# Building the quadratic feature map behind the window attention instead of ahead of it, in a fused attention and mixture-of-experts layer

## Chip, cores and metric

The kernel runs on the 8 cores of one Trainium2 chip. Each core takes one of the 8 sequences (4096 tokens of width 1024) and all weights; the cores exchange nothing. The metric is the device time in microseconds (us) of the slowest core. Times in the profile are of that core, one execution.

## What is computed

One layer: an attention block, a layer norm, an expert block, a layer norm. The attention block has two kinds of heads side by side on the same q, k and v: a causal linear attention on a feature map phi, and a softmax attention over a window of 65 tokens.

```python
def taylor_feature_map(x):            # x: [..., 16]  ->  [..., 153]
    iu, ju = jnp.triu_indices(d)
    scale = jnp.where(iu == ju, 0.5, 1.0 / math.sqrt(2.0))
    quad = x[..., iu] * x[..., ju] * scale
    return jnp.concatenate([ones, x, quad], axis=-1)
h = rmsnorm(x, norm_w)
q, k, v = h @ Wq, h @ Wk, h @ Wv                    # 16 heads of 64
q_phi, k_phi = taylor_feature_map(q @ Wqf), taylor_feature_map(k @ Wkf)
lin = linear_attention_causal(q_phi, k_phi, v)      # chunks of 128, carried state kv
win = sliding_window_attention(q, k, v)             # keys t-64 to t
x = layernorm(x + x + concatenate([lin, win]) @ Wout)
# then, with E=8 experts and TOP_K=2 of them per token:
# h0 = x w0, h1 = x w1, out = sum over chosen e of g_e * (h0 * silu(h1)) w2
x = layernorm(x + moe(x))
```

## The kernel before

A core works in four quarters of 1024 tokens. A quarter has two superchunks of 512 tokens (`superchunk`, line 364) and then the expert part (`phase_B`, line 854) over its 1024 tokens. A superchunk normalises four chunks of 128 tokens, transposes them, makes q, k and v of all four (192 matmuls of 128x512), and calls `chunk_attn` (line 469) for each of its four chunks. So there are 32 calls.

`Plan.op` (line 49) appends one instruction to the queue of its engine. An engine runs its queue strictly in the order in which the program emitted it. DVE, ACT and POOL instructions also wait for the one before on their own engine, and `after=[...]` names what else an instruction waits for, by counting semaphores. So the order in the source is the order on every engine. All rows of the profile have line 90, that of the helper; they are told apart by tile and shape. Most tiles of the attention part are carved out of one buffer and so are all named `arena`.

A call of `chunk_attn` emits, in this order:

- POOL copies q of this chunk into `q_pad` (lines 485 to 489); it waits for the last scores of the window attention of the chunk before (`prev_qpad_read`).
- PE projects q and k of the chunk on the 16 features (lines 491 to 504), DVE copies them out as `qf_tm` and `kf_tm`.
- `emit_tail` (line 769) for the chunk before: DVE copies the state to bf16, PE transposes the concatenated heads, ACT evacuates them, PE runs the output projection into `pbA` (32 matmuls 128x512), DVE adds it to the residual `t1`, and the layer norm follows in four passes of 1024 columns on ACT with small steps of DVE between the first ones. The first chunk of a quarter has no tail ahead of it.
- The phi build (lines 511 to 557): DVE scales `qf_tm` and `kf_tm` by 1/sqrt(2) into `qf_h` and `kf_h`, sets the ones, copies the linear terms, and multiplies the 15 groups of mixed terms, for q and k at once. POOL makes the 32 groups of squares (the diagonal terms, each 128x16), which wait for the second scaling `t_sc`; an `engine_nop` closes them and gives the token `t_phig`.
- The window attention (lines 561 to 625), in four groups of four heads: scores of the chunk's own keys into `pb3` and of the keys before into `pb6` (PE), two exponentials (ACT), two masks (POOL, `maskC` and `maskP`), the products with v into `pbB` (PE), a reciprocal and a multiplication (DVE). The exponentials of a group wait for the products of the group before (`prev_yw`), since `eC` and `eP` exist once.
- The linear attention (lines 630 to 724), again in four groups: PE transposes phi of q and of k into `pT`, which waits for `t_phi` and `t_phig`, ACT evacuates it, PE makes the scores, DVE masks them, PE makes the output and the state update, DVE normalises and adds.

The lines that set the hand-overs named above:

```python
t_sc = tsc("vector", self.kf_h[:, :], self.kf_tm[:, :], INV_SQRT2, None, ALU.mult, inc="v")
OP("gpsimd", "tensor_tensor", k3d[:, :, off:off + 1], khh3[:, :, i:i + 1],
   khh3[:, :, i:i + 1], ALU.mult, after=[t_sc, self.prev_kd])
teCm = OP("gpsimd", "tensor_tensor", ..., ALU.mult, after=[teC])
ttr = OP("tensor", "transpose", ..., after=[t_phi, t_phig, self.lr["pT"], self.prev_yl])
```

Of the kernel before, what the change touches and what calls it, by code (L numbers as in the profile page):

```python
# [14 lines left out]
NH = 16  # L15
FEAT = 16
# [7 lines left out]
INV_SQRT2 = float(1.0 / np.sqrt(2.0))  # L24
# [102 lines left out]
class Builder:  # L127
# [341 lines left out]
    def chunk_attn(self, S, c, C, tk_q, tk_k, tk_v):  # L469
        OP, tsc = self.OP, self.tsc  # L470
# [5 lines left out]
        def kslice(h_or_sl, width=128, prev=False, whole_slice=True, off=0):  # L476
# [10 lines left out]
           after=[tk_q[0], tk_q[1], self.prev_qpad_read])  # L487
# [3 lines left out]
        for sl in range(8):  # L491
# [6 lines left out]
                    after=[tk1], inc="v")  # L498
# [9 lines left out]
        self.emit_tail()  # L508
        if self.castage < 1:
            return  # L510
        tsc("vector", self.qf_h[:, :], self.qf_tm[:, :], INV_SQRT2, None, ALU.mult,
            after=[self.prev_phig])
        t_sc = tsc("vector", self.kf_h[:, :], self.kf_tm[:, :], INV_SQRT2, None,
                   ALU.mult, inc="v")

        k3d = self.kphi.rearrange("p (h w) -> p h w", h=NH)
        q3d = self.qphi.rearrange("p (h w) -> p h w", h=NH)
        ktm3 = self.kf_tm.rearrange("p (h w) -> p h w", h=NH)
        qtm3 = self.qf_tm.rearrange("p (h w) -> p h w", h=NH)
        khh3 = self.kf_h.rearrange("p (h w) -> p h w", h=NH)  # L520
        qhh3 = self.qf_h.rearrange("p (h w) -> p h w", h=NH)
        OP("vector", "memset", k3d[:, :, 0:1], 1.0, after=[self.prev_kd])
        OP("vector", "memset", q3d[:, :, 0:1], 1.0)
        OP("vector", "tensor_copy", k3d[:, :, 1:17], ktm3[:, :, :])
        OP("vector", "tensor_copy", q3d[:, :, 1:17], qtm3[:, :, :])
        import dataclasses as _dc
        def _two_sided(ap_k, ap_q):
            d = ap_q.offset - ap_k.offset
            return bass.AP(tensor=ap_k.tensor, offset=ap_k.offset,
                           ap=[list(p) for p in ap_k.ap[:1]] +  # L530
                              [[d, 2]] + [list(p) for p in ap_k.ap[1:]])
        off = 17
        t_phiv = None
        for i in range(FEAT):
            n = FEAT - i
            if n > 1:
                outv = _two_sided(k3d[:, :, off + 1:off + n],
                                  q3d[:, :, off + 1:off + n])
                in0v = _two_sided(
                    khh3[:, :, i:i + 1].broadcast_to([128, NH, n - 1]),  # L540
                    qhh3[:, :, i:i + 1].broadcast_to([128, NH, n - 1]))
                in1v = _two_sided(ktm3[:, :, i + 1:FEAT], qtm3[:, :, i + 1:FEAT])
                t_phiv = OP("vector", "tensor_tensor", outv, in0v, in1v, ALU.mult,
                            inc=("v" if i == FEAT - 2 else None))
            off += n
        off = 17
        for i in range(FEAT):
            n = FEAT - i
            OP("gpsimd", "tensor_tensor", k3d[:, :, off:off + 1],
               khh3[:, :, i:i + 1], khh3[:, :, i:i + 1], ALU.mult,  # L550
               after=[t_sc, self.prev_kd])
            OP("gpsimd", "tensor_tensor", q3d[:, :, off:off + 1],
               qhh3[:, :, i:i + 1], qhh3[:, :, i:i + 1], ALU.mult)
            off += n
        t_phig = OP("gpsimd", "engine_nop")
        self.prev_phig = t_phig
        t_phi = t_phiv

        if self.castage < 2:
            return  # L560
        win_toks = []
        for hg in range(4):
            hs4 = [4 * hg + j for j in range(4)]
            tsC = None
            for j, h in enumerate(hs4):
                tsC = OP("tensor", "matmul", self.pb3[:, 128 * j:128 * (j + 1)],
                         kslice(h // 2), self.q_pad[:, 128 * h:128 * (h + 1)],
                         start=True, stop=True,
                         after=[tqp, tk_k[0], tk_k[1], self.lr["pb3"]],
                         inc=("t" if j == 3 else None))  # L570
            teC = OP("scalar", "activation", self.eC[:, :], self.pb3[:, :],
                     AF.Exp, scale=WIN_SCALE, after=[tsC, self.prev_yw], inc="s")
            teCm = OP("gpsimd", "tensor_tensor",
                      self.eC.rearrange("p (j w) -> p j w", j=4),
                      self.eC.rearrange("p (j w) -> p j w", j=4),
                      self.maskC[:, :].unsqueeze(1).broadcast_to([128, 4, 128]),
                      ALU.mult, after=[teC])
            self.lr["pb3"] = teCm
            tePm = None
            if C > 0:  # L580
                tsP = None
                for j, h in enumerate(hs4):
                    tsP = OP("tensor", "matmul",
                             self.pb6[:, 128 * j:128 * (j + 1)],
                             kslice(h // 2, prev=True),
                             self.q_pad[:, 128 * h:128 * (h + 1)],
                             start=True, stop=True,
                             after=[self.lr["pb6"],
                                    self.ktail_tok if first_c else None],
                             inc=("t" if j == 3 else None))  # L590
                teP = OP("scalar", "activation", self.eP[:, :], self.pb6[:, :],
                         AF.Exp, scale=WIN_SCALE, after=[tsP, self.prev_yw], inc="s")
                tePm = OP("gpsimd", "tensor_tensor",
                          self.eP.rearrange("p (j w) -> p j w", j=4),
                          self.eP.rearrange("p (j w) -> p j w", j=4),
                          self.maskP[:, :].unsqueeze(1).broadcast_to([128, 4, 128]),
                          ALU.mult, after=[teP])
                self.lr["pb6"] = tePm
            self.prev_qpad_read = tsP if C > 0 else tsC
            tyw = None  # L600
            for j, h in enumerate(hs4):
                tk = OP("tensor", "matmul", self.pbB[:, 512 + 65 * j:512 + 65 * (j + 1)],
                        self.eC[:, 128 * j:128 * (j + 1)], vr[:, 65 * h:65 * (h + 1)],
                        start=True, stop=(C == 0),
                        after=[teCm, tk_v[0], tk_v[1], self.lr["pbB"]],
                        inc=("t" if (C == 0 and j == 3) else None))
                if C > 0:
                    tk = OP("tensor", "matmul", self.pbB[:, 512 + 65 * j:512 + 65 * (j + 1)],
                            self.eP[:, 128 * j:128 * (j + 1)],
                            vprev[:, 65 * h:65 * (h + 1)],  # L610
                            start=False, stop=True,
                            after=[tePm, self.vtail_tok if first_c else None],
                            inc=("t" if j == 3 else None))
                tyw = tk
            self.prev_yw = tyw
            zwin = self.pbB[:, 512:772].rearrange("p (j w) -> p j w", w=65)[:, :, 64:65]
            rcw = OP("vector", "reciprocal", self.smal[:, 16:20], zwin.squeeze(2),
                     after=[tyw], inc="v")
            c3 = self.concat.rearrange("p (half h w) -> p half h w", half=2, w=64)
            tnw = OP("vector", "tensor_tensor", c3[:, 1, 4 * hg:4 * hg + 4, :],  # L620
                     self.pbB[:, 512:772].rearrange("p (j w) -> p j w", w=65)[:, :, 0:64],
                     self.smal[:, 16:20].unsqueeze(2).broadcast_to([128, 4, 64]),
                     ALU.mult, after=[rcw, self.prev_ct], inc="v")
            self.lr["pbB"] = tnw
            win_toks.append(tnw)
        if self.castage < 5:
            return
        concat_last = None
# [101 lines left out]
    def OP(self, *a, **k):  # L730
        return self.pl.op(*a, **k)

    def tsc(self, eng, out, in0, s1, s2, op0, op1=None, after=(), inc=None, accum=None):
        if accum is not None:
            return self.OP(eng, "tensor_scalar", out, in0, s1, None, op0, op1,
                           accum_out=accum, after=after, inc=inc)
        if op1 is None:
            return self.OP(eng, "tensor_scalar", out, in0, s1, None, op0,
                           after=after, inc=inc)
        return self.OP(eng, "tensor_scalar", out, in0, s1, s2, op0, op1,  # L740
                       after=after, inc=inc)
# [444 lines left out]
```

How the kernel before makes its waits and increments, by code:

```python
        def f(e, waits=waits, meth=meth, args=args, kw=kw, incname=incname, incn=incn):  # L87
            for s, v in waits:
                e.wait_ge(sems[s], v)
            r = getattr(e, meth)(*args, **kw)
            if incname is not None:
                r.then_inc(sems[incname], incn)
# [16 lines left out]
        def f(e, waits=waits, fn=fn):  # L109
            for s, v in waits:
                e.wait_ge(sems[s], v)
            fn(e)
```

## Time and profile before

| what | us |
|---|---|
| median of 4 runs | 9538.18 |
| lowest and highest of them | 9407.78, 9975.75 |
| the profiled execution | 9407.96 |
| its span, slowest core (the others 9390.2 to 9403.5) | 9406.4 |
| PE busy in the span | 7036.7 (75%) |
| ACT, DVE, POOL busy | 2686.1, 1830.2, 871.6 |

Busy time of PE is an upper bound of its work, as matmuls are pipelined. The shares are means over two very different parts, attention and experts, so that a stage has to be read by itself. In the rows below, a row of the timeline has the start in us from the span's start, the length in us, the engine, line and operation, output and inputs with shapes, the number of merged instructions, and in brackets how long the engine had been idle before and what released it.

### The profile page before, as it was taken

How to read it: one execution, taken by the hardware profiler on the slowest of the kernel's cores; microseconds unless marked ns; L12 is line 12 of the kernel's file. 1: busy time of each engine (PE TensorE's matmuls, PEld its weight loads, DVE VectorE, ACT ScalarE, POOL GpSimd, SP SyncE). 2: the span in 40 equal slices, each digit the busy share in tenths (PEclk: the TensorE clock that was granted, in tenths of full speed). 3: DMA queues.
4: the chain of work that ended last, by engine and by line, in shares of the span. 5: the costliest groups of instructions: out<-in, count | busy, mean ns of one | idle time of the engine just before them, and what ended most of it. 6: DMA issues, size and time to landing. Idle time of an engine off the chain costs nothing.

```text
span 9406.4 us, 104878 instructions; the slowest of 8 cores (9390.2 to 9406.4 us)
## 1 busy us (share of the span) xinstructions
PE 7036.7 (75%) x37091; PEld 3423.8 (36%) x37091; DVE 1830.2 (19%) x4145; ACT 2686.1 (29%) x3885; POOL 871.6 (9%) x1533
## 2 busy tenths in 40 slices
PE   3344799999434479999944448999993444999998
PEld 1222344444222234444422223444442222444443
DVE  2222211111222221111122222111112222111111
ACT  1222233334222223333422222333342222233334
POOL 1212000000121100000012110000001111000000
PEclk8565899999656589999965659999996565999999
DMA  3000554643300054463420006355342001535442
GB/s 59 1 10 1 86 80 61 96 64 64 63 1 10 1 92 74 71 95 55 72 56 1 10 5 99 62 81 85 57 83 43 4 2 17 94 55 91 74 69 60
DMA packets 244417, 493.81 MB, mean 52 GB/s; under 512 B 14528, under 2 KB 14528, under 8 KB 243904
## 3 DMA queue, kind: packets, MB, share of 16 engines
q0 software_dynamic: 225472, 453.02, 31.0%
q1 hardware_dynamic: 18432, 34.09, 1.2%
q8 instruction: 305, 5.00, 0.2%
q14 instruction: 208, 1.70, 0.1%
HBM read 923.32 MB, written 16.78 MB: 100 GB/s over the span
## 4 chain that ended last, share of the span: by engine, by line
PE 71%; ACT 9%; POOL 7%; issue 5%; DVE 5%; DMA 2%; DVEq 0%; ACTq 0%; POOLq 0%; SPq 0%
PE pb L90 40%; PE pbA L90 16%; PE pbB L90 11%; ACT arena L90 8%; POOL arena L90 7%; PE pT L90 4%; DVE arena L90 3%; DMA arena<-x 1%; DVE t L90 1%; ACT t L90 1%; DVE smal L90 1%; DMA arena<-gb 1%; ACT smal L90 0%; DVEq L89 0%; ACTq L89 0%
## 5 line engine op out<-in xcount | busy, mean ns | idle before, releaser
L90 PE MATMUL pb<-arena 128*128 128x512 bf16 (+2 forms) x19328 | 3896.7, 364 | 305.2 <-ACT arena L90 257.7
L90 PEld LDWEIGHTS pb<-arena 128*128 128x128 bf16 (+1 forms) x19328 | 1850.5, 103 | 2323.4 <-issue 393.5
L90 ACT ACTIVATE arena<-pb,arena 128x512 bf16<-128x512 f32 x2048 | 1407.3, 687 | 2147.9 <-PE pb L90 2050.4
L90 PE MATMUL pbB<-arena 128*128 128x512 bf16 (+1 forms) x5504 | 1088.7, 342 | 1104.3 <-POOL arena L90 973.5
L90 PE MATMUL pbA<-arena 128*128 128x512 bf16 x6656 | 1554.7, 395 | 50.3 <-ACT arena L90 42.2
L90 DVE TENSOR_TENSOR arena<-arena 128x512 bf16<-128x512 bf16 (+13 forms) x1536 | 654.0, 426 | 3150.7 <-ACT arena L90 2951.7
L90 PEld LDWEIGHTS pbB<-arena 128*128 128x128 bf16 x5504 | 527.6, 104 | 1655.8 <-issue 1172.5
L90 PEld LDWEIGHTS pbA<-arena 128*128 128x128 bf16 x6656 | 670.9, 101 | 903.8 <-issue 180.1
L90 PE MATMUL pT<-idbf,arena 128*128 128x128 bf16 (+1 forms) x3072 | 415.7, 303 | 649.4 <-DVE arena L90 404.8
L90 ACT ACTIVATE arena<-pT 128x512 bf16<-128x512 bf16 (+1 forms) x576 | 368.7, 640 | 1269.6 <-PE pT L90 1245.8
L90 DVE TENSOR_TENSOR t<-t,arena 128x1024 f32<-128x1024 f32 x256 | 313.6, 1225 | 1553.7 <-ACT arena L90 1553.7
L90 PEld LDWEIGHTS pT<-idbf,arena 128*128 128x128 bf16 (+1 forms) x3072 | 272.2, 130 | 764.0 <-issue 754.8
L90 POOL TENSOR_TENSOR arena<-arena 128x16 bf16<-128x16 f32 x1024 | 340.1, 332 | 1815.2 <-DVE arena L90 1670.7
L90 POOL DMA_DIRECT2D arena<-w0t x64 | 57.1, 893 | 4199.4 <-PE pb L90 3957.2
L90 ACT ACTIVATE arena<-pb 128x512 bf16<-128x512 f32 x252 | 150.5, 597 | 926.9 <-PE pb L90 912.6
L90 ACT ACTIVATE arena<-pbA,arena 128x1024 f32<-128x1024 f32 x128 | 142.6, 1114 | 720.1 <-PE pbA L90 719.4
L90 ACT ACTIVATE arena<-pbB,arena 128x1024 f32<-128x1024 f32 x128 | 142.6, 1114 | 701.9 <-PE pbB L90 700.4
L90 DVE TENSOR_TENSOR arena<-pb,maskL 128x512 bf16<-128x512 f32 x128 | 88.5, 691 | 702.1 <-PE pb L90 702.1
L90 ACT ACTIVATE arena<-t 128x1024 bf16<-128x1024 f32 x64 | 67.6, 1056 | 392.6 <-DVE t L90 392.6
L90 DVE CAST arena<-pbA 128x512 bf16<-128x512 f32 x192 | 132.9, 692 | 226.0 <-PE pbA L90 226.0
L90 POOL TENSOR_TENSOR arena<-arena,maskC 128x512 bf16<-128x512 bf16 x128 | 147.2, 1150 | 207.9 <-ACT arena L90 198.5
L90 ACT ACTIVATE arena<-t,smal 128x1024 bf16<-128x1024 f32 (+1 forms) x128 | 146.9, 1148 | 36.8 <-DVE smal L90 30.8
(84 smaller groups left out, 1755.7 us busy)
## 6 DMA issues: line engine op xcount, KB each, us to landing
arena<-w2t POOLq DMA_DIRECT2D x32, 4352.0 KB, 31.6
arena<-w0t POOLq DMA_DIRECT2D x64, 2048.0 KB, 18.2
arena<-w1t POOLq DMA_DIRECT2D x64, 2048.0 KB, 28.3
arena<-x SPq DMA_DIRECT2D x32, 512.0 KB, 3.7
out<-t SPq DMA_DIRECT2D x32, 512.0 KB, 2.7
arena<-wout POOLq DMA_DIRECT2D x6, 2048.0 KB, 55.9
arena<-wq POOLq DMA_DIRECT2D x4, 2048.0 KB, 17.8
arena<-wk POOLq DMA_DIRECT2D x4, 2048.0 KB, 33.3
```

The source lines that it names most:

```text
L90: r = getattr(e, meth)(*args, **kw)
```

## The change

The phi build moves from ahead of the window attention to behind it, as one block. No instruction, token or buffer is changed. The tail of the chunk before stays where it was, ahead of both.

```diff
@@ -508,54 +508,6 @@
         self.emit_tail()
         if self.castage < 1:
             return
-        tsc("vector", self.qf_h[:, :], self.qf_tm[:, :], INV_SQRT2, None, ALU.mult,
-            after=[self.prev_phig])
-        t_sc = tsc("vector", self.kf_h[:, :], self.kf_tm[:, :], INV_SQRT2, None,
-                   ALU.mult, inc="v")
...
-        t_phig = OP("gpsimd", "engine_nop")
-        self.prev_phig = t_phig
-        t_phi = t_phiv
-
         if self.castage < 2:
             return
         win_toks = []
@@ -623,6 +575,53 @@
                      ALU.mult, after=[rcw, self.prev_ct], inc="v")
             self.lr["pbB"] = tnw
             win_toks.append(tnw)
+        tsc("vector", self.qf_h[:, :], self.qf_tm[:, :], INV_SQRT2, None, ALU.mult,
+            after=[self.prev_phig])
+        t_sc = tsc("vector", self.kf_h[:, :], self.kf_tm[:, :], INV_SQRT2, None,
+                   ALU.mult, inc="v")
...
+        t_phig = OP("gpsimd", "engine_nop")
+        self.prev_phig = t_phig
+        t_phi = t_phiv
         if self.castage < 5:
             return
```

POOL's queue in the second chunk of the kernel, before. The two copies are `q_pad`, the 32 instructions of 128x16 the squares, `ISA` the nop behind them, and maskC and maskP the masks of the four groups; the last copies are those of the chunk after:

```order
L90 COPY arena<-arena 64x8x128 x2
L90 TENSOR_TENSOR arena<-arena 128x16 x32
L90 ISA
L90 TENSOR_TENSOR arena<-arena,maskC 128x512
L90 TENSOR_TENSOR arena<-arena,maskP 128x512
L90 TENSOR_TENSOR arena<-arena,maskC 128x512
L90 TENSOR_TENSOR arena<-arena,maskP 128x512
L90 TENSOR_TENSOR arena<-arena,maskC 128x512
L90 TENSOR_TENSOR arena<-arena,maskP 128x512
L90 TENSOR_TENSOR arena<-arena,maskC 128x512
L90 TENSOR_TENSOR arena<-arena,maskP 128x512
L90 COPY arena<-arena 64x8x128 x2
```

And the same stretch of POOL's queue now:

```order
L90 COPY arena<-arena 64x8x128 x2
L90 TENSOR_TENSOR arena<-arena,maskC 128x512
L90 TENSOR_TENSOR arena<-arena,maskP 128x512
L90 TENSOR_TENSOR arena<-arena,maskC 128x512
L90 TENSOR_TENSOR arena<-arena,maskP 128x512
L90 TENSOR_TENSOR arena<-arena,maskC 128x512
L90 TENSOR_TENSOR arena<-arena,maskP 128x512
L90 TENSOR_TENSOR arena<-arena,maskC 128x512
L90 TENSOR_TENSOR arena<-arena,maskP 128x512
L90 TENSOR_TENSOR arena<-arena 128x16 x32
L90 ISA
L90 COPY arena<-arena 64x8x128 x2
```

The squares and their nop moved from ahead of the first mask to behind the last one, and stand now between the masks and the next chunk's copies.

DVE's queue in the same chunk, now. The 128x1024 addition is the residual of the tail, the pairs on `pbB` are the four normalisations of the window, the rows from the scaling (TENSOR_SCALAR 128x256) on are the phi build:

```order
L90 TENSOR_TENSOR t<-t,pbA 128x1024
L90 TENSOR_SCALAR smal<-smal 128x1 x2
L90 RECIPROCAL smal<-pbB 128x4
L90 TENSOR_TENSOR arena<-pbB,smal 128x256
...
L90 RECIPROCAL smal<-pbB 128x4
L90 TENSOR_TENSOR arena<-pbB,smal 128x256
L90 TENSOR_SCALAR arena<-arena 128x256 x2
L90 MEMSET arena 128x16 x2
L90 CAST arena<-arena 128x16x16 x2
L90 TENSOR_TENSOR arena<-arena 128x2x16x15
```

Before, the rows from the scaling on stood directly behind the two small TENSOR_SCALAR of the layer norm, and the four pairs on `pbB` behind the last product. PE's and ACT's queues are the same before and now.

## Rows read from the trace of the kernel before

**Rows 1.** The page, granted TensorE clock in 40 slices of the span, in tenths

```profile
PEclk8565899999656589999965659999996565999999
```

**Rows 2.** Busy time by stage: PE, PEld, DVE, ACT, POOL, then PEclk, DMA share, GB/s

```profile
0.00:964.00 964.00, 391.38 (x2859) 232.41 (x2859) 253.85 (x583) 200.06 (x317) 181.97 (x353) 0.64 0.10 17
964.00:2352.00 1388.00, 1337.26 (x6248) 608.43 (x6249) 209.60 (x456) 442.89 (x613) 35.98 (x38) 0.98 0.49 76
```

**Rows 3.** Who waited for whom, whole span: us in total, times, longest us

```profile
PE pbB L90 <- POOL arena L90: 1001.4, 252, 22.4
```

**Rows 4.** Timeline, 413 to 432, a chunk with a tail ahead

```profile
413.23 10.00 PE L90 MATMUL pbA<-arena 128*128 128x512 bf16 x32 [1.32 <-ACT arena L90]
...
423.06 0.61 PE L90 MATMUL pb<-arena 128*128 128x128 bf16 x8
...
428.07 0.69 DVE L90 TENSOR_SCALAR arena<-arena 128x256 f32<-128x256 f32 x2
...
429.03 15.10 POOL L90 TENSOR_TENSOR arena<-arena 128x16 bf16<-128x16 f32 x32 [57.62 <-DVE arena L90]
...
430.19 8.13 DVE L90 TENSOR_TENSOR arena<-arena 128x480 bf16<-128x480 f32 x15
431.18 1.29 ACT L90 ACTIVATE arena<-pb 128x512 bf16<-128x512 f32 x2
```

**Rows 5.** Timeline, 444 to 462, the window attention of the same chunk

```profile
444.43 1.15 POOL L90 TENSOR_TENSOR arena<-arena,maskC 128x512 bf16<-128x512 bf16 x1 [0.29 <-POOLq L90]
...
445.72 0.21 PE L90 MATMUL pbB<-arena 128*128 128x65 bf16 x1 [22.05 <-POOL arena L90]
...
447.37 1.04 PE L90 MATMUL pb<-arena 128*128 128x128 bf16 x8
...
448.13 1.29 ACT L90 ACTIVATE arena<-pb 128x512 bf16<-128x512 f32 x2 [15.67 <-PE pb L90]
448.93 1.15 POOL L90 TENSOR_TENSOR arena<-arena,maskC 128x512 bf16<-128x512 bf16 x1 [2.07 <-ACT arena L90]
...
460.89 1.15 PE L90 MATMUL pT<-idbf,arena 128*128 128x128 bf16 x8
461.26 0.18 DVE L90 RECIPROCAL smal<-pbB 128x4 f32<-128x4 f32 x1 [3.80 <-PE pbB L90]
...
461.55 0.42 DVE L90 TENSOR_TENSOR arena<-pbB,smal 128x256 bf16<-128x256 f32 x1
```

**Rows 6.** Timeline, 7879 to 7893, the same place in the last such chunk

```profile
7879.06 1.29 ACT L90 ACTIVATE arena<-pb 128x512 bf16<-128x512 f32 x2
7892.31 1.15 POOL L90 TENSOR_TENSOR arena<-arena,maskC 128x512 bf16<-128x512 bf16 x1 [0.29 <-POOLq L90]
```

**Rows 7.** Timeline, 159 to 189, the first chunk, without a tail ahead

```profile
159.94 0.60 ACT L90 ACTIVATE arena<-pb 128x512 bf16<-128x512 f32 x1 [48.55 <-PE pb L90]
...
176.34 1.15 POOL L90 TENSOR_TENSOR arena<-arena,maskC 128x512 bf16<-128x512 bf16 x1 [0.30 <-POOLq L90]
...
186.99 2.20 POOL L90 COPY arena<-arena 64x1024 bf16<-64x1024 bf16 x2
...
187.29 1.15 PE L90 MATMUL pT<-idbf,arena 128*128 128x128 bf16 x8
...
187.95 0.42 DVE L90 TENSOR_TENSOR arena<-pbB,smal 128x256 bf16<-128x256 f32 x1
```

**Rows 8.** Busy time in stretches of 2 us, columns as in rows 2

```profile
424.00:426.00 2.00, 0.00 (x0) 0.00 (x0) 0.62 (x1) 1.15 (x2) 0.00 (x0) 1.00 0.00 0
426.00:428.00 2.00, 0.00 (x0) 0.00 (x0) 0.31 (x2) 1.24 (x2) 0.00 (x0) 0.50 0.00 0
...
430.00:432.00 2.00, 0.00 (x0) 0.00 (x0) 1.69 (x4) 1.82 (x3) 1.57 (x4) 0.50 0.00 0
...
440.00:442.00 2.00, 0.00 (x0) 0.00 (x0) 0.00 (x0) 0.00 (x0) 1.28 (x6) 0.50 0.00 0
```

**Rows 9.** Timeline of PE, 5437, the shortest output projection

```profile
5437.48 8.39 PE L90 MATMUL pbA<-arena 128*128 128x512 bf16 x32 [1.32 <-ACT arena L90]
```

More of the change, by code:

```diff
@@ L510, in chunk_attn @@
             return
-        tsc("vector", self.qf_h[:, :], self.qf_tm[:, :], INV_SQRT2, None, ALU.mult,
-            after=[self.prev_phig])
-        t_sc = tsc("vector", self.kf_h[:, :], self.kf_tm[:, :], INV_SQRT2, None,
-                   ALU.mult, inc="v")
[L516 to L554, printed above, removed]
-        t_phig = OP("gpsimd", "engine_nop")
-        self.prev_phig = t_phig
-        t_phi = t_phiv
@@ L625, in chunk_attn @@
             win_toks.append(tnw)
+        tsc("vector", self.qf_h[:, :], self.qf_tm[:, :], INV_SQRT2, None, ALU.mult,
+            after=[self.prev_phig])
+        t_sc = tsc("vector", self.kf_h[:, :], self.kf_tm[:, :], INV_SQRT2, None,
+                   ALU.mult, inc="v")
+        k3d = self.kphi.rearrange("p (h w) -> p h w", h=NH)
+        q3d = self.qphi.rearrange("p (h w) -> p h w", h=NH)
+        ktm3 = self.kf_tm.rearrange("p (h w) -> p h w", h=NH)
+        qtm3 = self.qf_tm.rearrange("p (h w) -> p h w", h=NH)
@@ new lines, in chunk_attn, with _two_sided @@
+        khh3 = self.kf_h.rearrange("p (h w) -> p h w", h=NH)
+        qhh3 = self.qf_h.rearrange("p (h w) -> p h w", h=NH)
+        OP("vector", "memset", k3d[:, :, 0:1], 1.0, after=[self.prev_kd])
+        OP("vector", "memset", q3d[:, :, 0:1], 1.0)
+        OP("vector", "tensor_copy", k3d[:, :, 1:17], ktm3[:, :, :])
+        OP("vector", "tensor_copy", q3d[:, :, 1:17], qtm3[:, :, :])
+        import dataclasses as _dc
+        def _two_sided(ap_k, ap_q):
+            d = ap_q.offset - ap_k.offset
+            return bass.AP(tensor=ap_k.tensor, offset=ap_k.offset,
+                           ap=[list(p) for p in ap_k.ap[:1]] +
+                              [[d, 2]] + [list(p) for p in ap_k.ap[1:]])
@@ new lines, in chunk_attn @@
+        off = 17
+        t_phiv = None
+        for i in range(FEAT):
+            n = FEAT - i
+            if n > 1:
+                outv = _two_sided(k3d[:, :, off + 1:off + n],
+                                  q3d[:, :, off + 1:off + n])
+                in0v = _two_sided(
+                    khh3[:, :, i:i + 1].broadcast_to([128, NH, n - 1]),
+                    qhh3[:, :, i:i + 1].broadcast_to([128, NH, n - 1]))
+                in1v = _two_sided(ktm3[:, :, i + 1:FEAT], qtm3[:, :, i + 1:FEAT])
+                t_phiv = OP("vector", "tensor_tensor", outv, in0v, in1v, ALU.mult,
+                            inc=("v" if i == FEAT - 2 else None))
+            off += n
@@ new lines, in chunk_attn @@
+        off = 17
+        for i in range(FEAT):
+            n = FEAT - i
+            OP("gpsimd", "tensor_tensor", k3d[:, :, off:off + 1],
+               khh3[:, :, i:i + 1], khh3[:, :, i:i + 1], ALU.mult,
+               after=[t_sc, self.prev_kd])
+            OP("gpsimd", "tensor_tensor", q3d[:, :, off:off + 1],
+               qhh3[:, :, i:i + 1], qhh3[:, :, i:i + 1], ALU.mult)
+            off += n
+        t_phig = OP("gpsimd", "engine_nop")
+        self.prev_phig = t_phig
+        t_phi = t_phiv
```

## The prediction

> **What bounds the kernel now.** I began with the row of the granted TensorE clock over the whole span [rows 1]. It swings four times between values near 0.5 and long runs of 9: the four quarters of the tokens, each with an attention part, in which TensorE mostly waits, and an expert part, in which it does not. The two stretches of the first quarter say it in numbers [rows 2]: in the attention part (0 to 964 us, with the start of the kernel in it) PE is busy 391.38 of 964 us at a clock of 0.64, in the expert part 1337.26 of 1388 us at 0.98. The change touches only the attention part, so the question is what PE waits for there. The waits of the core answer for the place at issue [rows 3]: the matmuls into pbB wait for POOL 252 times, 1001.4 us in all, 22.4 us at the longest.
>
> The timeline of one chunk (the one whose output projection starts at 413.23) shows where such a wait comes from [rows 4]. PE runs the 32 matmuls of the output projection of the chunk before, then at 423.06 the eight scores of the first group of heads of this chunk. Then it stands still. DVE adds the residual, the layer norm goes to and fro between ACT and DVE, and only at 428.07 does DVE begin the phi build of this chunk. POOL takes its 32 squares (the diagonal terms of phi) from 429.03 to 444.13 (15.10 us). Beside it DVE's fifteen products (8.13 us from 430.19) are done by 438.32. The exponentials of the first group lie ready at 431.18 + 1.29 = 432.47, but their mask stands behind the squares in POOL's queue and starts at 444.43 [rows 5]. PE meets the first masked tile at 445.72, after 22.05 us of waiting. From there the window attention goes at 4.50 us a group (444.43 to 448.93). The fourth group frees PE at 460.89, where the first transposes of phi start at once: phi has been ready for 16.8 us and nobody waits for it. DVE ends the window's last normalisation at 461.55 + 0.42 = 461.97.
>
> So before the change each chunk pays on its chain for the squares and then for the window; the layer norm on ACT hides only the beginning of the squares.
>
> **The change part by part.** No instruction is added or removed; 21 DVE instructions (2 scalings, 2 memsets, 2 copies, 15 products) and POOL's 32 squares with their closing nop go from ahead of the window's instructions to behind them, in all 32 chunks.
>
> Gain, the window starts earlier. In the other three groups a mask starts 0.80 us after its exponential starts (448.13 and 448.93) [rows 5]. With the squares out of the way the first mask can follow the exponential of 431.18 by the same 0.80, so at 431.98, not at 444.43: 12.45 us earlier. ACT, and not POOL, sets that start, because the exponentials stand behind four passes of the layer norm. The last chunk of the kernel gives 7892.31 - 7879.06 - 0.80 = 12.45 as well [rows 6]; I read all 28 chunks of this form and they lie between 12.37 and 12.83, so 12.45 is taken for each.
>
> Loss, the phi build comes after the window. The window takes 461.97 - 444.43 = 17.54 us from its first mask to its last normalisation, and DVE's queue lets no phi instruction pass that one. Then the chain to the first transpose is: 0.11 us until the first scaling (as 461.44 to 461.55 between two dependent DVE instructions), 0.96 from the first scaling to the first square (428.07 to 429.03), 15.10 for the squares, and 0.30 for the nop and the hand-over (444.13 to 444.43). That makes 16.47. DVE's own part of phi needs 438.32 - 428.07 = 10.25 us and stays hidden beside the squares; without this cover nothing changes, since both run together as before. Of what is late next: the transposes wait for POOL. DVE, ACT and PE have nothing else queued that could fill these 16 us, as the next instructions of all three are those of the linear attention.
>
> Before, the transposes started 460.89 - 444.43 = 16.46 us after the first mask. So a chunk with a projection ahead of it becomes longer by 17.54 + 16.47 - 16.46 - 12.45 = 5.10 us. Times 28: 142.8 us.
>
> Four chunks, the first of each quarter, have no projection and no layer norm ahead. There the exponential is out at 159.94 and the mask waits until 176.34, which gives 176.34 - 159.94 - 0.80 = 15.60 us of earlier start [rows 7]. First mask to last normalisation is 187.95 + 0.42 - 176.34 = 12.03, to the transposes 187.29 - 176.34 = 10.95. (This first one has no previous block of keys; with one both are 5.5 longer and their difference is the same.) The change costs 12.03 + 16.47 - 10.95 - 15.60 = 1.95 us each, 7.8 for the four.
>
> Sum: 142.8 + 7.8 = 150.6 us. The profiled execution took 9407.96 us, its span 9406.4 and 1.6 around it, so 9407.96 + 150.6 = 9558.6, or 9559 us, 1.6% more. The median of the four runs shown, 9538.18, lies 130 us above the profiled execution, which is among the two lowest. My point is for an execution like the profiled one, and the range has room for a median that lies above it again.
>
> **Terms that no row fixes.** The hand-over from POOL's nop to PE is not seen before, as phi is never awaited. Its nearest rows are 0.14 us (mask end 445.58 to PE 445.72) and, as a far end, the length of a mask, 1.15; I take the 0.30, which has the nop in it. The ends are worth -5 and +27 us over 32 chunks. The squares could take another time in their new place. While DVE's products run, POOL does 4 of them in 2 us, and once these have ended 6 in 2 us [rows 8]. All 32 at the fast rate would take 10.7 us, 4.4 less. But the products move with the squares and start at the same distance from them, so I take 15.10 and keep the other for a rival. The q_pad copies of the next chunk now stand behind the squares; they take 2.20 us [rows 7] and are needed only 50 us later. The output projection takes 10.00 us in one chunk and 8.39 in another [rows 4, 9], depending on where in it the clock rises. Its phase will fall otherwise in a kernel with other distances. Around the middle of 9.2 this is worth 0.8 us times 31, 25 us either way.
>
> **Two rules of the skill.** The granted clock falls from 1.00 to 0.50, from 2.4 to 1.2 GHz, between 424 and 428, shortly after PE's last score [rows 8], and it is 0.50 when the window resumes. The Trainium skill (TensorE: Matmul & The Clock Gate, Why this matters for your kernels) says the same, that idle gaps between bursts of matmuls bring the slow clock back; by it the shorter gap after the change, about 9.6 us in place of 22.05, is still long enough and gives back nothing, so it gives 9559 too.
>
> POOL's squares are slower beside DVE's two-input products than alone [rows 8]. The Trainium skill (GPSIMD Engine Reference, 8. Key points) names this: the two engines share SBUF interfaces and contend when DVE has two SBUF inputs. By it the squares cost 15.1 us wherever they run beside those products, and a change that moved the squares alone would have been the better one.
>
> **The rivals.** (A) Not slower: the squares no longer meet the products, because one engine starts later than the other in the new place, so they run at 6 in 2 us. Price -4.4 us times 32 = -141, which gives 9418 us, no change. For it: the measured two rates. Against: the semaphore that starts the squares is that of the second scaling, as before. It turns the sign from a saving of 4.7 us a chunk on.
>
> (B) The clock stays up over the shorter gap. Eight scores take 0.61 us at the full clock and 1.04 at half [rows 4, 5]; with half of that difference on the chain and as much for the products with v, 0.42 us a group, 1.7 a chunk, 54 in all: 9505 us. Against it is the fall seen in rows 8.
>
> (C) Clearly slower: PE sees phi only when the q_pad copies behind it in POOL's queue are done. In 24 chunks such copies follow; 24 x 2.2 = 53 us more give 9612, 2.2% over before. The limit of 2% (188 us, about what a measurement of this kernel can tell from no change) is passed from 1.2 us a chunk beyond my sum on, wherever they come from. Against: the nop that signals phi is queued ahead of the copies.
>
> (D) Nobody waits for phi even now, so only the gain stays: 28 x 12.45 + 4 x 15.60 = 411 us, which gives 8997. For it there is only that phi was early before; against it that the transposes read it and follow the window directly.
>
> (E) The change does not start the window earlier, since something else holds the first mask: 32 x 17.55 = 562 us lost, 9970. The exponential ready at 432.47 speaks against it.
>
> **How the numbers follow.** Forecast 0.73, A 0.07, B 0.05, C 0.10, D 0.03, E 0.02. The terms without a row reach from 9559 - 5 - 25 = 9529 to 9559 + 27 + 25 = 9611; C ends at the same place. At the top I add about 90 us for a median that lies above an execution like the profiled one (it lay 130 above here), and 30 at the bottom toward B. The range is 9500 to 9700. Faster by over 2% is D: 0.03. Slower by over 2% is C, E and 0.02 of the forecast's upper edge: 0.14. Within 2%: 0.83.
>
> **What would show it.** The first maskC of a chunk starts 0.8 us after its exponential and not 13 us; PE's wait for POOL ahead of the first products with v falls from 22 to about 9.6 us; a new wait of PE into pT for POOL of about 17 us (448.64 to 465.99 on this chunk's clock) appears, 32 times; the squares still take 15.1 us; the distance from one chunk to the next grows from some 91.5 to 96.6 us. The prediction is wrong if the squares come out nearer 11 us, if the window's step is no longer 4.5 us, or if the transposes start before POOL has ended.

## Result and the profile after

| | before | changed |
|---|---|---|
| median, us | 9716.46 (14 runs) | 9917.44 (10 runs) |
| lowest, us | 9407.16 | 9545.42 |
| highest, us | 21070.4 | 13298.51 |
| ratio, 95% interval | | 1.0142 [1.0119, 1.0165] |

The chunks became longer by almost exactly the sum of the prediction, and the ratio is 1.4% where 1.6% was forecast. The stated range of 9500 to 9700 us nevertheless missed the median of 9917.44. In more than half of the executions of either kernel the cores of one die, or of both, ran at a lower granted clock; the medians contain them, the ratios leave them out, and the times named below are of executions without it, of which five of the ten experiments have only one.

The profile of the changed kernel shown here is that of its repetition in the first experiment (9560.17 us, span 9558.6). First the waits of the whole span, in the columns of [rows 3]:

```profile
POOL arena L90 <- ACT arena L90: 1943.6, 128, 61.3
...
PE pbB L90 <- POOL arena L90: 588.3, 252, 10.0
PE pT L90 <- POOLq L90: 554.3, 32, 17.7
```

PE's wait ahead of the window's products with v, 1001.4 us in [rows 3], is 588.3 us, and the longest is 10.0 in place of 22.4. A new wait has come up that did not exist: 32 times, once in each chunk, PE waits for POOL's queue ahead of its transposes into `pT`, 554.3 us in all or 17.3 each. What the one line gave, 413 us, is less than what the other took. The first line shows what the masks wait for now, the exponentials on ACT: 128 times, all four groups of all 32 chunks, where it was 96 times before.

The timeline of the same chunk as in [rows 4, 5]:

```profile
452.40 1.29 ACT L90 ACTIVATE arena<-pb 128x512 bf16<-128x512 f32 x2
453.20 1.15 POOL L90 TENSOR_TENSOR arena<-arena,maskC 128x512 bf16<-128x512 bf16 x1 [59.95 <-ACT arena L90]
...
454.50 0.21 PE L90 MATMUL pbB<-arena 128*128 128x65 bf16 x1 [9.53 <-POOL arena L90]
...
456.14 1.04 PE L90 MATMUL pb<-arena 128*128 128x128 bf16 x8
...
457.71 1.15 POOL L90 TENSOR_TENSOR arena<-arena,maskC 128x512 bf16<-128x512 bf16 x1 [2.07 <-ACT arena L90]
...
470.32 0.42 DVE L90 TENSOR_TENSOR arena<-pbB,smal 128x256 bf16<-128x256 f32 x1
470.85 0.69 DVE L90 TENSOR_SCALAR arena<-arena 128x256 f32<-128x256 f32 x2
...
471.81 15.11 POOL L90 TENSOR_TENSOR arena<-arena 128x16 bf16<-128x16 f32 x32 [2.64 <-DVE arena L90]
...
472.97 8.14 DVE L90 TENSOR_TENSOR arena<-arena 128x480 bf16<-128x480 f32 x15
487.19 1.12 PE L90 MATMUL pT<-idbf,arena 128*128 128x128 bf16 x8 [17.33 <-POOLq L90]
```

The first mask follows its exponential after 0.80 us (13.25 before). The window takes its 17.54 us as before (453.20 to 470.74). The squares begin 0.96 us after the scaling and take 15.11. From the last normalisation to the first transpose it is 487.19 - 470.74 = 16.45 us, where the prediction had 16.47. From exponential to transpose the chunk takes 34.79 us, against 29.71 before. From the first mask of a chunk to that of the next, where both lie in one superchunk and have a tail ahead, it is 95.9 us on average (91.4 before); the prediction had 96.6 and some 91.5.

### The profile page after: what moved, and what is told of

It reads as the page before. It is cut to its first block, busy times and chain, and to the rows that moved or that the text cites. A ratio compares the mean times of both kernels' runs of the same rounds, so it can differ in the third digit from the quotient of the medians.

```text
span 9761.0 us, 104942 instructions; the slowest of 8 cores (9743.0 to 9761.0 us)
## 1 busy us (share of the span) xinstructions
PE 7263.1 (74%) x37091; PEld 3475.9 (36%) x37091; DVE 1830.8 (19%) x4145; ACT 2685.9 (28%) x3885; POOL 869.8 (9%) x1533
## 4 chain that ended last, share of the span: by engine, by line
PE 71%; ACT 9%; POOL 7%; issue 6%; DVE 5%; DMA 2%; DVEq 0%; ACTq 0%; POOLq 0%; SPq 0%
PE pb L90 40%; PE pbA L90 16%; PE pbB L90 11%; ACT arena L90 8%; POOL arena L90 7%; PE pT L90 4%; DVE arena L90 3%; DMA arena<-x 1%; ACT t L90 1%; DVE t L90 1%; DVE smal L90 1%; DMA arena<-gb 0%; ACT smal L90 0%; DVEq L89 0%; ACTq L89 0%
## 5 line engine op out<-in xcount | busy, mean ns | idle before, releaser
L90 PE MATMUL pb<-arena 128*128 128x512 bf16 (+2 forms) x19328 | 4050.4, 374 | 299.2 <-ACT arena L90 251.8
L90 PEld LDWEIGHTS pb<-arena 128*128 128x128 bf16 (+1 forms) x19328 | 1885.6, 105 | 2435.4 <-issue 893.7
L90 PE MATMUL pbB<-arena 128*128 128x512 bf16 (+1 forms) x5504 | 1125.0, 351 | 691.6 <-POOL arena L90 560.9
L90 PE MATMUL pbA<-arena 128*128 128x512 bf16 x6656 | 1581.6, 400 | 50.3 <-ACT arena L90 42.2
```

Of the source, the lines that this page charges most:

```text
L90: r = getattr(e, meth)(*args, **kw)
```

## The experiments

The distance "exponential to transpose" is read per chunk, from the first group's exponential on ACT to the first transpose into `pT` on PE, and averaged over those of the 28 chunks with a tail that could be read whole (22 to 27 of them, 17 in one). It was 29.81 us before. "The window" is the time from the first mask to the last normalisation.

### The changed kernel again

No edit.

> The changed kernel unaltered, for an undisturbed profile beside the other runs. Theory (the chain of a chunk is window, then squares): the first mask 0.80 us after its exponential, squares 15.1 us, exponential to first transpose 34.8 us where before it was 29.7, ratio 1.014 to 1.016. Rival (the new order costs nothing, the difference is other executions): exponential to transpose no longer than 29.7 us and ratio below 1.005.

Measured: lowest 9547.56, against 9407.14 for the kernel before beside it, ratio of the two 1.0149. Exponential to transpose 34.84 us on average, +5.03 a chunk, so 140.8 us in 28. The four chunks without a tail grew by 1.62, 1.66, 1.66 and 1.84 us, 6.8 in all (the first one from 27.35 to 28.97). Together 147.6 us. The theory holds, the rival falls.

The difference of the lowest times is 140 us, some 8 us less than the chunks give. The output projection supplies them. The 32 projections of a core, averaged over the eight cores of either profile, take 295.6 us in all before and 286.3 us here, and the granted clock during them averages 0.76 before and 0.78 here.

### The squares left out, in the old order

```diff
         for i in range(FEAT):
             n = FEAT - i
-            OP("gpsimd", "tensor_tensor", k3d[:, :, off:off + 1],
-               khh3[:, :, i:i + 1], khh3[:, :, i:i + 1], ALU.mult,
-               after=[t_sc, self.prev_kd])
-            OP("gpsimd", "tensor_tensor", q3d[:, :, off:off + 1],
-               qhh3[:, :, i:i + 1], qhh3[:, :, i:i + 1], ALU.mult)
+            if C % 8 == 0:
+                (the same two)
             off += n
```

> The order of before, POOL's squares left out in 28 of 32 chunks (kept in the first of each quarter; the output then has old diagonal terms). Theory (the squares hold the first mask, up to the exponential): mask 0.80 us after the exponential, window start 12.45 us earlier, 28 x 12.45 = 349 us less, about 9059, ratio 0.963. Rival (something else holds the mask, such as DVE's products): less than half of it, over 9230. The fifteen products of DVE, 8.13 us beside the squares, get shorter if the two engines slow each other: to 6 us or so; unchanged if only POOL suffers.

Measured: 9150.56 to 9155.95 in four runs, 257 us under the 9407.14 beside it, where 349 were expected; at 9150.56 us the rival (over 9230) falls too. The first mask does start 0.80 us after its exponential, so the squares alone had held it. But the window became longer, 21.18 us on average against 17.55. The chunk that starts at about 408:

```profile
409.62 11.33 DVE L90 TENSOR_TENSOR arena<-arena 128x480 bf16<-128x480 f32 x15
410.61 1.28 ACT L90 ACTIVATE arena<-pb 128x512 bf16<-128x512 f32 x2
411.41 1.31 POOL L90 TENSOR_TENSOR arena<-arena,maskC 128x512 bf16<-128x512 bf16 x1 [59.97 <-ACT arena L90]
...
421.05 0.18 DVE L90 RECIPROCAL smal<-pbB 128x4 f32<-128x4 f32 x1
421.34 0.42 DVE L90 TENSOR_TENSOR arena<-pbB,smal 128x256 bf16<-128x256 f32 x1
421.91 0.67 PE L90 MATMUL pbB<-arena 128*128 128x65 bf16 x8 [6.22 <-DVE arena L90]
```

DVE's products now lie in front of the window's first normalisation. They hold it until 421.05, and PE with its single `pbB` half waits 6.22 us for it. The products also take 11.33 us in place of 8.13, because the masks now run beside them (the run with the squares alone, below, shows it one by one). Neither stood in the theory, and they cost 3.63 us a chunk, which is the missing part: 28 x (12.5 - 3.6) = 249.

### The squares left out, in the new order

The same edit in the changed kernel.

> The changed order, the same squares left out. Theory (PE waits for POOL's squares, and DVE's part of 10.25 us is hidden under them): exponential to first transpose falls from 34.8 to about 28.8 us, 28 x 6 = 168 us less than the changed kernel, about 9378, ratio to before 0.997. If DVE's products get faster without POOL beside them, up to 2 us a chunk more, down to 9320. Rival (DVE's products, not the squares, end last): no gain, 9545.

Measured: lowest 9412.51, within 35 us of the expected 9378. Exponential to transpose 29.56 us on average, 5.3 less than with squares.

```profile
448.75 0.42 DVE L90 TENSOR_TENSOR arena<-pbB,smal 128x256 bf16<-128x256 f32 x1
449.28 0.69 DVE L90 TENSOR_SCALAR arena<-arena 128x256 f32<-128x256 f32 x2
...
451.40 8.13 DVE L90 TENSOR_TENSOR arena<-arena 128x480 bf16<-128x480 f32 x15
459.79 1.12 PE L90 MATMUL pT<-idbf,arena 128*128 128x128 bf16 x8 [11.50 <-DVE arena L90]
```

PE's wait for phi shrinks from 17.33 to 11.50 us and is now DVE's. So in the changed kernel the squares were what ended last, and DVE's part of 10.25 us was hidden under them. DVE's products take 8.13 us with POOL idle, exactly as beside the squares: the squares do not slow them. The rival falls.

The gain was to be 6 us a chunk. Of the 35 us that are missing, 13 lie in DVE's scaling. Where the squares stood, POOL now runs the next chunk's `q_pad` copies. In 20 of the 28 chunks the first scaling meets one and takes about 0.95 us in place of 0.29. In the chunk above it meets none, and the two scalings take 0.69 together:

```profile
2607.23 1.04 POOL L90 COPY arena<-arena 64x1024 bf16<-64x1024 bf16 x1
2607.47 0.95 DVE L90 TENSOR_SCALAR arena<-arena 128x256 f32<-128x256 f32 x1
```

### The whole phi build ahead of the tail

```diff
         self.lr["pb2"] = t_kftm
+        (the phi build, the same block)
         self.emit_tail()
```

> The whole phi build ahead of the tail of the chunk before, so that it runs beside the output projection. Theory (both orders lay the squares on the chain, and only the layer norm or the window covers a part): squares done by about 425 us on the clock of the chunk quoted, mask 0.80 us after the exponential, transposes with no wait behind the window, 28 x 12.45 = 349 us less than before, about 9059, ratio 0.963; the four chunks without a tail as before. Rival (DVE, busy with phi, makes the tail's residual addition late, or the squares slow ACT or PE): the projection to exponential distance grows and the gain is under 200 us.

Measured: lowest 9050.34, 356.8 us under the kernel before (9407.14), where 349 were expected; this is 3.8%. Exponential to transpose 17.28 us, that is 0.80 and the window. The build lies beside the output projection:

```profile
383.06 15.92 POOL L90 TENSOR_TENSOR arena<-arena 128x16 bf16<-128x16 f32 x32 [39.00 <-DVE arena L90]
...
384.22 8.15 DVE L90 TENSOR_TENSOR arena<-arena 128x480 bf16<-128x480 f32 x15
...
385.89 9.41 PE L90 MATMUL pbA<-arena 128*128 128x512 bf16 x32 [1.32 <-ACT arena L90]
392.46 1.50 DVE L90 CAST kvb<-kv 128x1040 bf16<-128x1040 f32 x2
...
395.48 1.22 DVE L90 TENSOR_TENSOR t<-t,pbA 128x1024 f32<-128x1024 f32 x1 [1.52 <-PE pbA L90]
...
403.26 1.29 ACT L90 ACTIVATE arena<-pb 128x512 bf16<-128x512 f32 x2
404.06 1.15 POOL L90 TENSOR_TENSOR arena<-arena,maskC 128x512 bf16<-128x512 bf16 x1 [5.09 <-ACT arena L90]
```

DVE is ready for the residual (its idle time before it is 1.52 us), the squares end at 398.98, and the mask waits 5.09 us for ACT only. From the start of the projection to the exponential it is 17.1 us on average, against 17.4 before, so the rival falls. In both earlier orders the squares were on the chain; this one takes them off it. The squares take 0.8 us more than in [rows 4]. Two of them meet DVE's copies of the state (the CAST above) and take 0.67 and 0.66 us in place of 0.26, which is all of it. The first of the two:

```profile
392.46 0.70 DVE L90 CAST kvb<-kv 128x1040 bf16<-128x1040 f32 x1
392.61 0.67 POOL L90 TENSOR_TENSOR arena<-arena 128x16 bf16<-128x16 f32 x1
```

### The squares after the products, alone on their engines

```diff
-               after=[t_sc, self.prev_kd])
+               after=[t_phiv, self.prev_kd])
```

> The changed kernel, with the squares waiting for DVE's last product and no longer for the second scaling, so that they run alone. Theory (the products slow the squares from 0.33 to about 0.5 us each): squares 10.7 us in place of 15.1, chain 10.25 + 10.7 in place of 15.1 + 0.96, exponential to transpose 39.9 us, 32 x 5.2 = 166 us more than the changed kernel, about 9711, ratio to before 1.032. Rival (15.1 us is the squares' own time wherever they stand): 44.5 us, 9850, ratio 1.047.

Measured: lowest 9787.35, between the two. Exponential to transpose 42.31 us, +7.5 on the changed kernel. The squares of the chunk:

```profile
483.68 8.13 DVE L90 TENSOR_TENSOR arena<-arena 128x480 bf16<-128x480 f32 x15
492.07 12.88 POOL L90 TENSOR_TENSOR arena<-arena 128x16 bf16<-128x16 f32 x32 [12.20 <-DVE arena L90]
505.22 1.12 PE L90 MATMUL pT<-idbf,arena 128*128 128x128 bf16 x8 [24.66 <-POOLq L90]
```

Neither theory had the size right. Alone the squares take 12.88 us and not 10.7; beside the products 15.1. The products slow them, but by 2.2 us and not 4.4. Grouped by shape (count, busy us, mean ns of one), first this kernel from 490 to 506 and then the kernel before from 429 to 444:

```profile
L90 POOL TENSOR_TENSOR arena<-arena 128x16 bf16<-128x16 f32 x32 | 8.4, 264 | 16.6 <-DVE arena L90 12.2
```

```profile
L90 POOL TENSOR_TENSOR arena<-arena 128x16 bf16<-128x16 f32 x32 | 10.7, 333 | 62.1 <-DVE arena L90 57.6
```

A square is 264 ns alone and 333 ns on average beside the products, and between two squares there is a gap of (12.88 - 8.4)/31 = 0.14 us in either case. Half of the squares of a chunk meet a product. They take 395 ns on average, the others 269. Taken singly in the kernel before, a square beside the widest product and one beside a middle one:

```profile
430.19 0.66 DVE L90 TENSOR_TENSOR arena<-arena 128x480 bf16<-128x480 f32 x1
430.36 0.61 POOL L90 TENSOR_TENSOR arena<-arena 128x16 bf16<-128x16 f32 x1
...
434.29 0.46 DVE L90 TENSOR_TENSOR arena<-arena 128x288 bf16<-128x288 f32 x1
434.44 0.42 POOL L90 TENSOR_TENSOR arena<-arena 128x16 bf16<-128x16 f32 x1
```

Each square ends 0.12 us behind the product beside which it began (430.97 and 430.85), or 0.11 (434.86 and 434.75). So squares and products go in step, one by one, and while the products are the longer of the two, the product sets how long a square takes, and not the square's own 16 columns. The prediction's 10.7 us came from "6 in 2 us" in [rows 8]; such a row counts every instruction that touches its stretch, those cut at its edges too, so 5 in 2 us was the rate.

### The squares alone behind the window

The squares and their nop moved, DVE's part of the phi build where it was before.

```diff
         t_phiv = ... (DVE's part stays ahead of the window)
-        off = 17 ... OP("gpsimd", "tensor_tensor", ...)   # squares, nop
         (window attention)
+        off = 17 ... OP("gpsimd", "tensor_tensor", ...)   # squares, nop
```

> DVE's part of the phi build where it was before, only POOL's squares and their nop behind the window. Theory (squares without products beside them take 10.7 us, and behind the window they need not wait for DVE): in the 28 chunks with a tail exponential to transpose about 28.5 us against 29.7 before, in the four others the products hold up the first normalisation and cost some 2 us each; 9380 to 9420, ratio 0.998 to 1.001, and 1.3% under the changed kernel. Rival (15.1 us wherever they stand): exponential to transpose 33 us, 9500 or more.

Measured: 9549.64, the same as the changed kernel, and a miss of 130 us or more for the theory. The squares do run alone in 12.88 us and do not wait for DVE, and exponential to transpose is 33.77 us, 1.1 less than in the changed kernel; the four chunks without a tail are 1.9 to 2.9 us longer than there. But the window takes 21.16 us, as in the run without squares in the old order. Grouped by shape, DVE from 441.6 to 453, one product of each width:

```profile
L90 DVE TENSOR_TENSOR arena<-arena 128x384 bf16<-128x384 f32 x1 | 1.3, 1319 | 0.1
L90 DVE TENSOR_TENSOR arena<-arena 128x352 bf16<-128x352 f32 x1 | 1.3, 1282 | 0.1
L90 DVE TENSOR_TENSOR arena<-arena 128x224 bf16<-128x224 f32 x1 | 1.3, 1276 | 0.1
L90 DVE TENSOR_TENSOR arena<-arena 128x192 bf16<-128x192 f32 x1 | 1.2, 1160 | 0.1
L90 DVE TENSOR_TENSOR arena<-arena 128x480 bf16<-128x480 f32 x1 | 0.7, 659 | 0.1
```

And two of the same widths in the kernel before:

```profile
L90 DVE TENSOR_TENSOR arena<-arena 128x384 bf16<-128x384 f32 x1 | 0.6, 562 | 0.1
...
L90 DVE TENSOR_TENSOR arena<-arena 128x224 bf16<-128x224 f32 x1 | 0.4, 396 | 0.1
```

Four of the fifteen products, as many as there are masks beside them, take 1.16 to 1.32 us in place of 0.37 to 0.56; the widest, before the first mask, keeps its 0.66. The masks beside them take 1.31 and 1.28 us in place of 1.15. A product that meets a mask ends only 0.2 to 0.4 us behind the mask, about 0.8 us late, 3.2 us for the four. That makes the products 11.32 us long, and the window's first normalisation waits behind them. The changed kernel is free of this, since no product runs beside a mask in it.

### The layer norm between the groups of the window

The version with the phi build first, in which `emit_tail` hands its layer norm out in four pieces (sum; variance; rsqrt and centring; scaling), each emitted behind the scores of one group of the window.

```diff
             self.prev_qpad_read = tsP if C > 0 else tsC
+            if self.ln_steps:
+                self.ln_steps.pop(0)()
```

> The phi build ahead of the tail, and the tail's layer norm given out in four pieces, one behind the scores of each group of the window, and no longer ahead of the first exponential. Theory (with the squares out of the way ACT's layer norm sets the start of the window): the first mask then waits for the squares' end at 425.4, not for the exponential at 431.2, 6.3 us earlier, 28 x 6.3 = 176 us less than the version with the phi build first alone, about 8880, ratio 0.944. Rival (the four passes lengthen the window by what they save ahead of it, since the step from one group to the next grows over 4.5 us): no gain over that version, 9059.

Measured: lowest 8926.7, ratio to before 0.9492 [0.947, 0.9513], 124 us under the version without it; 176 were expected. The exponential comes 9.1 us after the projection's start in place of 17.1, and the window keeps its 17.60 us, so the passes fit between the exponentials and the rival falls. The mask then waits for the squares, 4.05 us behind the exponential on average:

```profile
374.90 15.95 POOL L90 TENSOR_TENSOR arena<-arena 128x16 bf16<-128x16 f32 x32 [38.98 <-DVE arena L90]
...
387.51 1.29 ACT L90 ACTIVATE arena<-pb 128x512 bf16<-128x512 f32 x2 [9.91 <-PE pb L90]
...
391.14 1.15 POOL L90 TENSOR_TENSOR arena<-arena,maskC 128x512 bf16<-128x512 bf16 x1 [0.29 <-POOLq L90]
```

The trace of the version without it had this gain in it: there the mask starts 4.64 us behind the end of the squares on average, here 0.29, and 28 x 4.35 = 122. The 6.3 us of the theory were read from the kernel before. The squares take 15.95 us here, 0.85 more than in [rows 4], because of the two that meet the copies of the state, and that is part of the 52 us missing.

### Paired squares, in three orders

One POOL instruction makes the square of k and of q (128x32), 16 in place of 32.

```diff
-            OP("gpsimd", "tensor_tensor", k3d[:, :, off:off + 1], khh3..., khh3..., ALU.mult, ...)
-            OP("gpsimd", "tensor_tensor", q3d[:, :, off:off + 1], qhh3..., qhh3..., ALU.mult)
+            dg = _two_sided(khh3[:, :, i:i + 1], qhh3[:, :, i:i + 1])
+            OP("gpsimd", "tensor_tensor",
+               _two_sided(k3d[:, :, off:off + 1], q3d[:, :, off:off + 1]),
+               dg, dg, ALU.mult, after=[t_sc, self.prev_kd])
```

> The order of before, with each square of k and of q made by one POOL instruction of 128x32 in place of two of 128x16: 16 instructions. Theory (on POOL a square costs by the instruction, not by its elements): squares about 8 us in place of 15.1, the first mask 7 us earlier in all 32 chunks, 225 us less than before, about 9180, ratio 0.976. Rival (it costs by the element): squares 13 us or more, over 9340.

> The changed order with the same 16 paired squares. Theory (with the squares under DVE's 10.25 us, DVE's products end last, as in the run of this order without squares): exponential to first transpose 29.6 us in place of 34.8, in all 32 chunks, 5.2 x 32 = 166 us less than the changed kernel, about 9380, ratio 0.997; so the changed order is then behind the order of before by 200 us, more than with single squares, since in it none of DVE's products is hidden. Rival (cost by the element): 9545 as before the pairing.

> The phi build ahead of the tail, the layer norm given out behind the scores, and the 16 paired squares. Theory: in the version without the pairs the first mask still waited 4.05 us for the end of the squares (mask to exponential, mean of the chunks read); with them it starts 0.8 us after the exponential, 3.25 x 28 = 91 us less than 8927, and some 28 us in the four chunks without a tail, about 8810, ratio 0.937. Rival (the layer norm's first pass, or the scores' release, then holds the window): no gain over 8927.

Measured, lowest of each, with 9407.11 for the kernel before beside them: old order 9215.51, new order 9377.17 (ratio 0.997 [0.995, 0.9989]), the version with the build first and the layer norm spread 8820.5. POOL and the transpose in the new order:

```profile
443.08 8.86 POOL L90 TENSOR_TENSOR arena<-arena 128x32 bf16<-128x32 f32 x16 [2.64 <-DVE arena L90]
...
444.24 8.13 DVE L90 TENSOR_TENSOR arena<-arena 128x480 bf16<-128x480 f32 x15
452.63 1.12 PE L90 MATMUL pT<-idbf,arena 128*128 128x128 bf16 x8 [11.50 <-DVE arena L90]
```

Twice the elements in half the instructions take 8.86 us in place of 15.1, so here a square costs mostly by the instruction. The old order gained 191.6 us where 225 were expected, the new one 168 where 166 were, the last version 106 where 119 were; the three rivals fall. In the new order DVE's products end last again (11.50 us of wait, as without squares). In the old order the mask comes 7.05 us behind its exponential in place of 13.3, which is 6.3 us a chunk. With cheap squares the new order is behind the old one by 9377 - 9216 = 162 us. In the last version the mask starts 0.80 us after its exponential, and the whole is 6.2% faster than the kernel before.

## Why the prediction came out as it did

**What bounds the kernel.** Right. PE waited for POOL's masks, and these for the squares: with the squares left out in the old order the mask follows its exponential by 0.80 us.

**The gain of 12.45 us.** Right. The distance from exponential to mask fell from 13.25 to 0.80 us, and ACT's layer norm then sets the start: in the order with the phi build first, spreading the layer norm took another 124 us off the kernel.

**The loss of 17.54 + 16.47 us.** Right to 0.02 us in the chunk shown. DVE's 10.25 us were hidden under the squares, as claimed: without the squares 5.3 us a chunk come back, and no more.

**The sum of 150.6 us.** A little high. The chunks with a tail give 140.8 and the four others 6.8, 147.6 together, against 142.8 and 7.8. The lowest times differ by 138 to 140 us. The part left, some 8 us, is the output projection, which takes 9.3 us less in all (295.6 and 286.3 us for the 32, average of the cores). That is the term that I had bounded by 25 us either way and set to nothing. No run changes it by itself; why the clock stands higher during it in the new order stays open.

**The range.** This is the step that failed: "about 90 us for a median that lies above an execution like the profiled one (it lay 130 above here)". The median of the ten runs lies 372 us above the lowest of them (9917.44 and 9545.42), and that of the kernel before came out 309 above its own. Two of the four times shown already stood 260 and 568 us above the lowest, so a median of a few draws from such a spread could lie anywhere between; an allowance of 90 us did not say that. The kernel before has a spread of the same kind, so it is not the change that makes it. For an execution like the profiled one the point of 9559 lies 14 us above the lowest measured, and the change stayed within 2%, to which the prediction gave 0.83.

**The hand-over.** 0.27 us from the squares' end (486.92) to the transpose (487.19); 0.30 was taken. So rival C, a release held until the copies behind the nop, is refuted.

**Rival A and the rule on shared interfaces.** Rival A did not happen: the squares still met the products and took 15.11 us. Of the rule behind it the direction was right, the size was not. Beside the products the squares take 15.1 us and alone 12.88, so 2.2 us a chunk and not 4.4, from a count that took cut instructions as whole. The aside that moving the squares alone "would have been the better one" is wrong: it came out at 9549.64, no better than the changed kernel, because the products then meet the masks, which hold them up as the squares do not. In the changed kernel squares and products kept their distance and the 15.1 us stood, as forecast.

**Rival B, the clock.** In the chunks with a tail the window keeps 17.54 us, its eight scores take 1.04 us, and the granted clock is 0.50 from 452 to 458 us, so the clock did not stay up over the gap of 9.53 us. This agrees with the fall seen in [rows 8], and with the rule that the prediction cites from the Trainium skill (TensorE: Matmul & The Clock Gate, Why this matters for your kernels), that idle gaps between bursts of matmuls bring the slow clock back. **D and E** are refuted by the new wait of 17.3 us, 32 times, and by the mask 0.80 us behind its exponential.

## What to carry to other kernels

Moving a block behind the work that it delays pays only if something else covers it in the new place; compare the two covers, not the wait removed with nothing. Here 12.45 us of early start were bought with 17.5, while the place that cost nothing was further ahead, beside the output projection, where POOL and DVE had been idle. Ask also what the moved instructions will then run beside: the squares alone behind the window left the products to the masks, which cost 3.6 us a chunk. A wait on an in-order engine names the queue to look at: the mask waited for work that nobody needed yet.

## What the runs showed of the hardware

- When one of the squares, masks or copies on POOL meets a DVE instruction that reads and writes `arena`, or DVE's copy of the state, the one that began later ends only after the other. A square that begins 0.17 us into the widest product ends 0.12 us behind it (0.61 us in place of 0.26). A product that begins behind a mask of 128x512 ends 0.2 to 0.4 us behind the mask (1.32 us in place of 0.56). A scaling behind a `q_pad` copy takes 0.95 us in place of 0.29. The squares do not lengthen the products, 8.13 us for the fifteen with and without them, since each product began and ends first. The squares beside the residual addition, which reads `pbA`, keep their 0.26 us.
- On POOL a 128x16 multiplication takes 264 ns and a gap of 0.14 us. One of 128x32 that meets no product takes 0.34 us (the first of the paired squares). Beside the products it is 8.86 / 16 = 0.55 us with its gap, against 15.1 / 32 = 0.47 for one of 128x16 there: twice the elements for 17% more time.
- A row of busy time over a short stretch counts instructions that are cut at its edges. Rates should be taken from the length of a merged group divided by its count.
